# A two-layer gated cross-attention kernel: the step order of all engines is rewritten, first-layer keys go through DRAM, and ScalarE normalises in the second layer

## What is computed

```python
x = x + tanh(g_xattn[0]) * xattn0(layernorm(x), ctx, ctx)   # 16 heads of 8, biases on q, k, v
x = x + tanh(g_ffn[0])   * moe(layernorm(x))                # 8 experts, top 2, gelu, 512 hidden
x = x + tanh(g_xattn[1]) * xattn1(ctx, ctx, layernorm(x))   # no biases, per-head weights, key mask
x = x + tanh(g_ffn[1])   * dense_moe(layernorm(x))          # 4 experts of 256, 1 to 4 used per token
```

## Time and profile before

| | |
|---|---|
| three runs | 1275.43, 1276.24 (median), 1279.92 us |
| the profiled execution | 1273.86 us, its span 1272.1 us |
| busy in the span | PE 85%, PE weight load 71%, DVE 71%, ACT 59%, POOL 43% |
| attention of layer 1 | first scores at 14.5 us, routing ends at about 422 us |
| its experts | to about 689 us |
| attention of layer 2 | first scores at 726.8 us, last of 32 groups from about 1037 us |
| its experts | to the end |

### The profile page before, as it was taken

The page is one execution under the profiler, slowest core; times in us unless marked ns, Lnnn a source line. Parts: engine busy times, 40 slices in busy tenths (PEclk is TensorE's granted clock), DMA queues, the critical chain, the costliest instruction groups (busy, mean ns, idle before and its releaser), DMA issues.

```text
span 1272.1 us, 40209 instructions
## 1 busy us (share of the span) xinstructions
PE 1085.7 (85%) x13845; PEld 898.6 (71%) x13845; DVE 905.7 (71%) x3061; ACT 756.2 (59%) x1629; POOL 543.2 (43%) x699
## 2 busy tenths in 40 slices
PE   6788888887674599999998788888888878999998
PEld 3566666665553399999998566666665657999997
DVE  4677877776674745454453378888888887998887
ACT  4788777786672155555554376677776774444443
POOL 2114544555635434444444466556555531222220
PEclk7999999999997699999999799999999998999999
DMA  6222211111100233333333121111111100000000
GB/s 189 82 77 93 66 44 47 50 52 46 50 31 32 81 88 98 92 95 95 95 95 89 33 49 43 47 43 45 45 45 42 40 7 1 26 18 23 19 22 26
DMA packets 116781, 71.89 MB, mean 57 GB/s; under 512 B 51736, under 2 KB 105240, under 8 KB 116632
## 3 DMA queue, kind: packets, MB, share of 16 engines
q1 hardware_dynamic: 108440, 53.13, 15.2%
q0 software_dynamic: 8192, 16.79, 4.3%
HBM read 45.88 MB, written 22.94 MB: 54 GB/s over the span
## 4 chain that ended last, share of the span: by engine, by line
PE 44%; issue 23%; POOL 15%; DVE 13%; SPq 3%; DMA 1%; ACT 0%; DVEq 0%; POOLq 0%; another core or an unknown queue 0%; ACTq 0%
PE ps_m L1773 10%; POOL w1a L658 8%; PE ps_p L1658 4%; PE ps_m L1658 4%; POOL rs L587 4%; DVE mx L996 3%; PE ps_s L1759 3%; PE ps_s L1760 3%; PE ps_s L1761 3%; PE ps_s L1490 3%; PE ps_s L1646 2%; PE ps_s L1648 2%; PE ps_s L1647 2%; PE ps_s L1589 2%; DVE Pr L1002 2%
## 5 line engine op out<-in xcount | busy, mean ns | idle before, releaser
L727 ACT ACTIVATE PT<-ps_p 128x512 f32<-128x512 f32 x320 | 187.6, 596 | 61.3 <-PE ps_p L1548 28.2
L996 DVE TENSOR_REDUCE mx<-ps_s 128x8 f32<-128x512 f32 x256 | 169.0, 680 | 44.8 <-PE ps_s L1490 44.8
L658 POOL DMA_INDIRECT w1a<-louts,gi x128 | 125.6, 981 | 121.0 <-DVE mx L996 53.0
L811 ACT ACTIVATE Kbd<-ps_s,c 128x512 f32<-128x512 f32 x128 | 87.8, 688 | 113.4 <-PE ps_s L1648 113.1
L1533 PE MATMUL ps_p<-cst,Pr 128*128 128x128 f32 x1024 | 146.4, 277 | 0.8 <-DVE orow L1268 0.4
L576 POOL TENSOR_TENSOR spare<-spare 1x1 f32<-1x1 f32 x99 | 21.3, 215 | 291.9 <-DVE b1s L1351 151.7
L1773 PE MATMUL ps_m<-xn3T 128*128 128x128 f32 x1136 | 137.9, 275 | 0.0
L1773 PEld LDWEIGHTS ps_m<-xn3T 128*128 128x128 f32 x1136 | 132.7, 192 | 0.0
L877 ACT ACTIVATE xn3T<-ps_s,b1s 128x256 f32<-128x256 f32 x284 | 111.5, 474 | 26.2 <-PE ps_s L1761 26.1
L616 POOL DMA_INDIRECT lists<-xn3T,pos x80 | 78.7, 984 | 103.1 <-DVE mx L996 77.2
L1533 PEld LDWEIGHTS ps_p<-cst,Pr 128*128 128x128 f32 x1024 | 120.0, 144 | 2.3 <-issue 0.9
(11 more groups left out here) (221 smaller groups left out, 2710.4 us busy)
## 6 DMA issues: line engine op xcount, KB each, us to landing
xn3T<-lists SPq DMA_DIRECT2D x71, 128.0 KB, 2.1
louts<-xn3T SPq DMA_DIRECT2D x71, 128.0 KB, 1.8
ctxg<-in_ctxT SPq DMA_DIRECT2D x32, 256.0 KB
Kbd<-in_ctxT SPq DMA_DIRECT2D x512, 8.0 KB
out<-x SPq DMA_DIRECT2D x16, 256.0 KB, 2.3
w1a<-in_L_ffn_W SPq DMA_DIRECT2D x8, 256.0 KB, 3.0
w2a<-in_L_ffn_W SPq DMA_DIRECT2D x8, 256.0 KB, 3.9
Pr<-in_ctxT SPq DMA_DIRECT2D x16, 128.0 KB, 2.4
```

The lines of the kernel that those rows point to most:

```text
L658: nc.gpsimd.indirect_dma_start(ysb[g.par][:, s_, t, :], None, louts, bass.IndirectOffsetOnAxis(ap=gi[g.par][:, c:c + 1], axis=0)).then_inc ...
L727: return nc.scalar.activation(dst, src, ACT.Copy)
L996: V.tensor_reduce(mx[g.par][:, q, :], per_key(ps_s[:, q, :]), AX, ALU.max).then_inc(max_done, 1)
```

## The change

- **Order.** On PE, `heads_back` moves from the end of a step to the start of the next (offset -1 to -2), and `scores` comes second, ahead of all turns. On DVE `denominators` and `heads` move to the start of the next step; bank 0 is taken first (maximum, then its subtraction at once), then 2, 3, 1 (`ORDER`); `residual` comes behind the subtractions. `logits` is last on PE, `tokens2_turned` later. ACT's exponentials follow the new order.
- **First-layer keys.** `keys` is now its own matmul, two groups ahead. ACT makes one copy (`kT`, with the bias) in place of four. SP stores it to a DRAM tensor `keys_kept` (128 KB, runs of 256 bytes) and a step later loads it into `Kbd` with 16 DMAs (`spread_keys`). Both `Kbd` are cleared by POOL at the start. `load_ctx` runs three groups ahead. All this is in SP's steps, behind the late loads.
- **First-layer values** go through bank 7 in place of a scores bank.
- **Second layer.** DVE computes -mean times inverse deviation (`shifts`, one small operation) in place of the four normalising operations; ACT normalises with four activations with scale and bias at the start of the next step. `logits` reads the copy of the tokens in `xn3T`, so that one copy of ACT goes.
- **POOL** makes the inverse deviations behind the second quarter of its scatters or gathers and no longer waits there for the subtractions.

The core of the diff:

```diff
-ORDER = (2, 3, 0, 1)
+ORDER = (0, 2, 3, 1)
...
+            def keep_keys(g):
+
+                sp.wait_ge(k_ready, g.count(1, 1))
+                sp.dma_start(keys_kept[g.k, :, :, 0, :], kT[:, :].rearrange("p (b k) -> p b k", b=4)).then_inc(k_kept, 16)
+
+            def spread_keys(g):
+
+                if g.k == 0:
+                    sp.wait_ge(kbd_clear, 1)
+                sp.wait_ge(k_kept, g.count(16, 16))
+                wait(sp, s_done, g.count(4, -4))
+                for h in range(H):
+                    rows = slice(DK * h, DK * h + DK)
+                    sp.dma_start(Kbd[g.par][rows, :, h % 4, :],
+                                 keys_kept[g.k, rows, :, 0, :]).then_inc(spread_in[g.par], 16)
+
             def step(g):
-                if g.plus(2).real() and (g.layer or g.k >= 0):
+                if g.layer == 0:
+                    if g.plus(1).real():
+                        spread_keys(g.plus(1))
+                    if g.plus(2).real():
+                        keep_keys(g.plus(2))
+                    if g.plus(3).real() and g.k >= -1:
+                        load_ctx(g.plus(3))
+                elif g.plus(2).real():
                     load_ctx(g.plus(2))
...
-                if have(0):
-                    pool.wait_ge(sub_done, g.count(2, 2))
-                rows_moved(2)
                 if have(-2) or have(2):
                     inverse_deviations(g)
+                rows_moved(2)
...
+            def normalise(g, slot, dst, step_, s_out):
+                act.wait_ge(nb_ready, step_.k + 3)
+                for j in range(2):
+                    nc.scalar.activation(dst[:, j, :], x[:, 2 * g.k + j, :], ACT.Identity, bias=nb[:, slot + j:slot + j + 1],
+                                         scale=rs[:, slot + j:slot + j + 1]).then_inc(s_out, 1)
...
+                if g.layer == 1:
+                    now(normalise_in, 1, g.plus(-1))
+                    now(normalise_mid, -3, g.plus(-1))
                 now(probs_out, -1, 0)
                 now(tokens_in, 1)
+                now(exps, 0, 0)
                 now(heads_out, -2)
                 now(probs_out, -1, 1)
+                now(queries, 1)
+                if g.layer == 0:
+                    now(keys, 2)
+                else:
+                    now(values, 0)
+                now(probs_out, -1, 2)
+                now(exps, 0, 2)
+                now(probs_out, -1, 3)
+                now(exps, 0, 3)
                 now(tokens2, -3)
...
                 now(exps, 0, 1)
+                now(sums_out, -1)
...
+                dve.wait_ge(ln_rs, ln_step(step_))
+                V.scalar_tensor_tensor(nb[:, :], mv[:, :, 0], -1.0, rs[:, :], ALU.mult, ALU.mult).then_inc(nb_ready, 1)
...
+                    now(denominators, -2)
+                    now(heads, -2)
                     now(statistics_in, 2)
+                    now(maximum, 0, 0)
+                    now(subtract, 0, 0)
                     now(maximum, 0, 2)
                     now(maximum, 0, 3)
                     now(high_maxima, 0)
...
+                    now(heads_back, -2)
+                    now(scores, 0)
                     now(probs_turned, -1, 0)
                     now(tokens_turned, 1)
                     now(heads_turned, -2)
                     now(probs_turned, -1, 1)
-                    now(scores, 0)
+                    now(keys, 2)
+                    now(queries, 1)
+                    now(project_out, -2)
```

More of the change, by code:

```diff
@@ L64, in constants @@
     c[1::32, C_IND + S:C_IND + P] = 1
-    for i in range(4):
-        c[:, C_BLK + i] = (np.arange(P) % 32) // DK == i
     c[:, C_DESC:C_DESC + E0] = E0 - np.arange(E0)
@@ L343, in build @@
         kept = PT[0]
-        kq_bank, lg_bank, rk_bank, v_bank = (ps_s[:, i, :] for i in range(4))
+        kq_bank, lg_bank, rk_bank = (ps_s[:, i, :] for i in range(3))
         ones_ready, arrays_in = sem("ones_ready"), sem("arrays_in")
@@ L354, in build @@
         kbd_in = [sem("kbd_in0"), sem("kbd_in1")]
+        spread_in = [sem("spread_in0"), sem("spread_in1")]
+        kbd_clear, k_done, k_ready, k_kept = (sem(n) for n in ("kbd_clear", "k_done", "k_ready", "k_kept"))
         folded_done, folded_ready, mask_clear = sem("folded_done"), sem("folded_ready"), sem("mask_clear")
@@ L425, in scores_read @@
             else:
[L426 removed]
+                pe.wait_ge(exp_done, last.count(4, q))
         def steps(eng, layer, step):
@@ L765, in exps, with keys, queries @@
                                      scale=SCALES[g.layer]).then_inc(exp_done, 1)
-            def keys_queries(g):
-                act.wait_ge(kq_done, g.count(1, 1))
-                wait(act, s_done, g.count(4, -4))
-                if g.layer == 0:
-                    copy(qT[g.par][:, :], kq_bank[:, GT:2 * GT], bcol[:, 0:1])
-                    for i in range(4):
-                        ins = nc.scalar.activation(Kbd[g.par][:, :, i, :], kq_bank[:, 0:GT].rearrange("p (b k) -> p b k", b=4),
-                                                   ACT.Identity, bias=bkm[:, i:i + 1], scale=blk[:, i:i + 1])
-                    ins.then_inc(kq_ready, 1)
-                else:
-                    copy(qT[g.par][:, :], kq_bank[:, GT:2 * GT]).then_inc(kq_ready, 1)
+            def keys(g):
+                act.wait_ge(k_done, g.count(1, 1))
+                wait(act, k_kept, g.count(16, 0))
+                copy(kT[:, :], kq_bank[:, 0:GT], bcol[:, 1:2]).then_inc(k_ready, 1)
+            def queries(g):
+                act.wait_ge(q_done, g.count(1, 1))
+                wait(act, s_done, g.count(4, -4))
+                copy(qT[g.par][:, :], kq_bank[:, GT:2 * GT], bcol[:, 0:1] if g.layer == 0 else None).then_inc(q_ready, 1)
             def values(g):
@@ L1242, in step @@
                     now(gate_logits, -3)
-                    now(normalise_in, 2, g)
-                    now(normalise_mid, -2, g)
                     now(gate_hidden, -3)
-                    now(denominators, -1)
+                    if have(-2) or have(2):
+                        shifts(g)
                     now(gate_depth, -3)
-                    now(heads, -1)
                     if g.k == GROUPS + 1:
@@ L1604, in logits @@
                 w = (wr0, wr1)[g.layer]
+                rows = xn3T[:, GT * g.k:GT * g.k + GT] if g.layer else xn2T[g.par][:, :]
                 n = w.shape[1]
```

137 lines of the change are left out of this document (62 added, 75 removed).

## The result

The changed kernel takes 1374.97 us (median of 4, 1373.87 to 1379.40) against 1275.84 us for the kernel before beside it, a ratio of 1.0778 (95% interval 1.0750 to 1.0807). It is 7.8% slower; I had forecast 1255, with 1282 as the upper end. The span of its profile is 1373.0 us, 100.9 more than before.

The account below looks back on a forecast made before the run. A ring of waits, no full engine, was taken to set each layer's step. First layer -11 and second -10 made -21 us on 1273.86, 1252.9; with the median 2.4 above, 1255 us, range 1228 to 1282.

Parts of the forecast that it names:

- The 16 loads have the shape of the second layer's, 6.9 us for all.: First layer, SP's queue: the key loads of a step would issue as the second layer's do, 6.9 us.
- SP's ring: First layer, per step: 16 loads 6.9 us, then a store that must land 2.4, together 9.3 us.
- The landing: First layer: the 128 KB store of keys in runs of 256 bytes lands 2.4 us after its issue.
- The rule that I had weighed against the change: Skill's warning on small runs and latency: each store lands 2 us later, SP's ring 11.3, total 1284 us.
- The head: First layer's start: first scores at about 41 us behind SP's queue, in place of 14.46; a loss of 26 us.
- SP is the clock: Rival, first layer: store lands after 4.8 us, SP's ring 11.7, head 42 us, total 1297 us; 14%.
- Layer 1's other steps: First layer: ring taken as 9.9 us, routing 0.7 per step more; twenty steps at 10.6, seven late at 10.9.
- The stall of the late steps: First layer: PE's stops in `values_by_probs` during POOL's scatters, 2.6 us in six steps, taken as gone.
- The rival that the stall turns up in the scores: Rival, first layer: PE's stall stays or turns up in scores during POOL's last scatters, 1270 us; 15%.
- ScalarE's ring of 9.6 us: Second layer, per step: ScalarE's ring is longest at 9.6 us against 10.0 before; 31 steps make -13 us.
- ACT is the bound: Rival, second layer: shift late, activations 0.57 us each and uncovered, steps stay 10.0, total 1268 us; 17%.
- more is hidden: Rival, both layers: routing falls into other waits, ACT's pieces overlap better, steps 9.9 and 9.2, total 1224 us; 12%.

Follow-up runs that it names:

- e16: Changed kernel with only the DRAM tensor of the kept keys laid out partition outermost, run beside a kernel before of 1277.6 us: 1298.76 us, ratio 1.0156.
- e2: Changed kernel with the kept keys laid out partition outermost and layer 2's exponential of bank 0 two places later: 1281.37 us in one run.
- e15: Changed kernel with partition-outermost keys, late layer-2 exponential, groups 0 and 1's keys by ScalarE, group 2's context between mask loads: 1266.59 us, ratio 0.9906.
- e14: Changed kernel with POOL's order of layer 2 as before the change: 1353.57 us, ratio 1.0596.
- e5: Changed kernel with only the kept keys laid out partition outermost, in the set where before took 1243.24 us: 1238.13 us, ratio 0.9960.
- e10: The changed kernel run again unedited, with a profile: 1378.72 us, ratio 1.0790.
- e3: Changed kernel with keys spread from SBUF without a DRAM tensor; in layer 2 late exponential and PE's first turn before scores: 1505.25 us in one run.
- e12: The program of e15 with POOL's four scatters or gathers of a step in one run, in both layers: 1327.54 us, ratio 1.0403.
- e4: Changed kernel with the 15 late loads issued from POOL's queue in place of SP's: 1374.15 us in one run.

## Why the prediction was wrong

The miss on the span is 100.9 + 21 = 122 us. By its own steps:

- **"The 16 loads have the shape of the second layer's, 6.9 us for all."** The step that failed. They have its bytes, runs and destination, but not its source pattern: 11.04 us. SP's ring is 13.4 where I had 9.3, and SP became the first layer's clock. The layout alone is worth 74 of the 122 us. The Trainium skill ("Perfetto Trace Analysis", What "DMA-bound" means) says that a queue solid with DMA slices is busy generating descriptors, not moving data; the trace agrees as far as it goes: the DMA engines are at 0.23 while SP issues for 12.2 of each 13.4 us.
- **The landing** was right: 2.4 us. The rule that I had weighed against the change ("DMA: Bandwidth & Descriptors" of the Trainium skill, Specifications and "Latency and other measured facts": runs under 512 bytes, up to 2 us of latency) would have made it 4.4 by my estimate; the stores between 260 and 280 us do not show it.
- **The head**: right in kind, first scores at 44.98 in place of 40.8, because of the same 4.3 us of loads.
- **The rival "SP is the clock"** is what happened, at 14%, but I had priced it by a late store, 11.7 us. The issue time I took as known, and it had no bounds.
- **Layer 1's other steps.** With the layout mended (e16) 31 steps take 350.1, not 327.4: 23 us of the miss. Steps without routing are 10.6 where I had 9.9. Routing adds 3.0 us in four steps (10.59, 11.86, 12.08 and 10.85), where I had 2.8. Late steps are 12.1 where I had 10.9. I had removed DVE's wait of 0.92 for the logits; but they are now the last matmuls of PE's step, and in e2 the wait is three times as long:

```profile
178.86 0.17 DVE L1083 COPY lgb<-ps_s 128x16 f32<-128x16 f32 x1 [2.91 <-PE ps_s L1660]
```

  The logits lie in a bank of the scores, so the next scores wait for this copy (`lg_read`), and in a step that routes for `rank` too (`rank_read`), which VectorE reads from a scores bank. Both orders have these waits in their code; in the new one they hold PE up. In e16, scores in a step that routes (`rank` ends 0.3 us before them) and in the next:

```profile
257.47 1.81 PE L1533 MATMUL ps_s<-Kbd,qT 32*64 32x256 f32 x32 [1.71 <-issue]
...
268.02 1.12 PE L1533 MATMUL ps_s<-Kbd,qT 32*64 32x256 f32 x32 [0.18 <-DVE lgb L1080]
```

- **PE's clock** was a term that I put at nothing. In e16 PE waits 1.7 to 2.0 us ahead of its scores seven times; behind five of these waits the granted clock is 0.50 (the lower of its two levels, 1.2 GHz) for some us, here from 257.5 to 261, and the scores take 1.81 to 2.02 us in place of 1.12. The step with the first of the rows above, and the next (columns as above):

```profile
247.98:261.93 13.95, 11.68 (x166) 9.67 (x166) 10.54 (x41) 7.04 (x17) 5.92 (x7) 0.77 0.21 57
261.93:272.77 10.84, 9.51 (x162) 7.39 (x161) 7.68 (x24) 7.58 (x18) 5.98 (x7) 1.00 0.29 76
```

  By an estimate, with 12.08 us for each, three such steps of e16 (12.89, 13.95 and 15.33 us, clock 0.92, 0.77 and 0.73) hold 6 of the 23 us; the steps of 12.08, at 0.86, have some of it too.

- **The stall of the late steps** is mostly gone, as forecast: 12.1 in place of 13.8. Single late steps still take 15 (15.33 in e16, 14.88 and 15.27 in e15), all at a granted clock of 0.73. The rival that the stall turns up in the scores came true in kind: PE stands before them, but by the waits above.
- **Layer 2**, the sum: ScalarE's ring of 9.6 us was right. e14 has 9.60, e5 too, and its parts fit: from the last copy of one step to the first of the next ScalarE spends 0.67 + 1.65 + 0.39 = 2.7 us on the wait for `nb`, normalising and the wait for PE (forecast 2.5 + 0.2), and 6.9 on the rest (forecast 6.9). What I left out is POOL: I priced the move of its quarters at nothing, and it put a gather where the scores' signal is due, 1.05 us in 25 of the 31 steps (e10 against e14: 322.8 and 297.7 us for 31).
- The rival "ACT is the bound", 10.0 us per step, did not happen: with ScalarE normalising e14 and e5 take 9.60. The rival "more is hidden" did not either.

Sum: 74 (layout) + 23 (layer 1's ring, with the clock) + 25 (gather) + 6 (head) = 128, less 6 that lie between the layers and at the end: 122.

Open: what in the chip makes an issue longer when the source's strides merge into one, since only the patterns were varied; why PE's signals are late during a gather in most sets and not in one, and what holds SP up behind the load of x. Shown is that moving the gather moves the time, not the path by which POOL holds up PE.

## What to carry to other kernels

The price of a DMA issue belongs to the pattern of both sides: take it from a row with the same pattern, or bound it by twice its value (here it was 2.2 times). When a queue with 16 issues per step carries the data of a ring, make it a rival of its own. When the order of an engine off the path is changed, ask where its indirect transfers will fall against the other engines' signals. Time that a new order frees on one engine is only gained if the piece it waits for next has not been moved to the end of another's step. When an engine comes out full in an experiment that was to free another, the experiment says nothing of the other: look at its busy time first.

## What was not expected of the hardware

- 8 x 4 runs of 256 bytes into 8 partitions: 301 ns of the issuing queue from a source with two strides (three layouts), 649 ns from one with a single even stride, 686 ns from contiguous SBUF rows. The context load behind them, itself unchanged, took 619 ns in place of 362.
- A gather of 0.97 us that is running when PE's last scores end delays their signal to VectorE by up to 1.0 us. Counted from the scores' start, the maximum comes 0.4 to 0.5 us behind the gather's end: at 2.2 with a gather from 0.82 to 1.79 (e10), at 2.0 with 0.61 to 1.58 (e3), at 1.8 with 0.34 to 1.31 (e2). With a gather that ends at 0.56 (e14), or one that starts at 1.05 (e15), it comes at 1.2, as without one. In e5 it comes at 1.2 beside a gather from 0.81 to 1.78.
- Four gathers in a row beside a dense run of small matmuls cost more than gathers spread over the step: 11.10 against 9.92 us per step (e12 and e15), with PE's granted clock at 0.93 against 0.98.
- Behind five of seven waits of PE of 1.7 to 2.0 us the granted clock was 0.50 for some us, and the same 32 matmuls took up to 2.02 us in place of 1.12 (e16, layer 1).
- Behind a load of 3.5 MB SP's next issue takes 11.4 us (a mask load, in the changed kernel) or 15.39 us (the store of keys, in e4), while the DMA engines have a share of 1.04 to 1.14; POOL's four mask loads issue in 3.47 us in that time.
